# Messages of the tensor-product layer inside the first 100 turns of the ODE's loop

## The chip, the cores and the metric

The kernel runs on one core of a Trainium2 chip. A core has a matrix engine (TensorE, PE in the profile), VectorE (DVE), ScalarE (ACT), GpSimd (POOL) and SyncE (SP, which here only issues DMAs), each with its own queue of instructions, and semaphores between them. The metric is the device time of one execution in microseconds; of several runs the median counts.

## The reference

Eight layers follow each other, each with a layer norm ahead and a residual sum behind: graph convolution, experts, an equivariant tensor-product message layer, an ODE, a second graph layer, an LSTM, a third graph layer, and a product-key layer. `x` has 625 rows (nodes) of 512; there are 20000 edges, sorted by their receiver. The two layers that matter:

```python
# layer 3, for every edge: h is a small MLP of 8 edge features, y of 4 edge attributes
tpw = h @ W_mlp4 / sqrt(64)                     # 64 -> 512, split in w1..w4 of 128
s0, s1 = x0[sender], x1[sender]                 # 128, 128 x 3
p1 = w1 * s0 * y0
p2 = (w2 * s0)[:, :, None] * y1[:, None, :]
p3 = w3[:, :, None] * s1 * y0[:, None, :]
p4 = w4 * einsum('eum,em->eu', s1, y1) / sqrt(3)
msg = segment_sum([p1, p4, p2, p3], receiver)   # 1024 a node
x = x + lin(msg) / 10
# layer 4: y0 is row 0 of the normed x; 624 steps of Runge-Kutta 4, one row of output each
f = lambda z: tanh(tanh(z @ W1.T + b1) @ W2.T + b2) @ W3.T + b3
k1 = f(y); k2 = f(y + dt/2*k1); k3 = f(y + dt/2*k2); k4 = f(y + dt*k3)
y = y + dt * (k1 + 2*k2 + 2*k3 + k4) / 6
```

The ODE is one chain on a single row. It reads of layer 3's result only row 0; its own output is added to all rows.

## The kernel before

**Messages.** Nodes lie in NT = 5 groups of TN = 125, edges in 160 tiles of TE = 125, four to a unit of 500. `stage_graph` finds for each group the first unit and the number of units that hold its receivers (`bounds`); a unit on a border is worked through for both groups. With these inputs the five groups take 19, 8, 7, 5 and 5 units, 44 units of 4 = 176 tiles. `stage_messages` (L664) runs once per group, one after the other. SyncE loads the MLP's output for two tiles (L700), GpSimd copies the sender numbers (L710) and gathers the senders' 512 values by an indirect DMA (L713), TensorE makes `tpw` (L734: 64 rows contracted, 125 x 512 out, f32), VectorE forms the products and the one-hot matrix of receivers (L773 to L792), ScalarE p2 (L754), and TensorE adds up: one-hot times products, two times 512 columns into two banks that keep the sum over the whole group (L725). TensorE alternates, product of this tile, sum of the tile before. Behind the five stages `stage_message_out` (L799) transposes the sums and multiplies them by the output weights.

**ODE.** `layer_ode` (L877) first loads and multiplies weights, so that a step is done on the hidden side: `ps_z`, `ps_u` and `ps_a` are columns of 128 values, and `tanh` of one gives the input of the next product. A sub-step s = 0..3 has two halves, A (ScalarE: `a = tanh(ps_z or ps_u)`, L1034 or L1037; TensorE: `W2 a`, L1003) and B (ScalarE: `b = tanh(ps_a)`, L1039; TensorE: `M b`). Each product is split in four matmuls of 32 output rows (`quarters`, L980), since TensorE can take a column in four 32-wide tiles. Between the halves, where TensorE would wait for ScalarE, `busy` (L985) runs zero matmuls of 384 (A) or 320 (B) columns, two rounds of four quarters; nobody reads their result. VectorE adds `zh`, `zf` (L1049, L1050) from `ps_z`, which TensorE needs in the B half of s = 0, 1 and 2, and forms `part`, `p` and `sums` (L1052 to L1058); `p` is needed by TensorE in the B half of s = 3. A turn of the loop has UN = 4 steps (16 sub-steps), there are 156 turns. All is in the order in which it is written: every engine has one queue, nothing reorders. In the same block SyncE and GpSimd split the LSTM's weights into f16 parts in pieces of 1024 columns (`split_weights`, L1089), with nothing but their own waits between pieces.

## Time and profile before

| | us |
|---|---|
| median of 3 runs (8022.19 to 8033.26) | 8031.54 |
| the profiled execution, its span | 8021.68, 8020.0 |
| five message stages | 453 to 1047.9 |
| output product of the messages | 1047.9 to 1072.8 |
| the ODE's loop | 1105.0 to 3868.9 |
| TensorE busy, VectorE, ScalarE, GpSimd | 7173.6 (89%), 2471.2 (31%), 1713.7 (21%), 697.0 (9%) |

A line of a group names source line, engine, operation, output<-inputs, the tile of the matrix engine (rows*columns), the shape, the count, then busy time and the mean of one in ns, then the idle time ahead and what ended it. A matmul in f32 leaves two records. `PEclk` or the granted clock is given as a share of full speed, 1.00 being 2.4 GHz and 0.50 1.2 GHz. "Busy" of TensorE counts the zero matmuls too. PEld is the loading of weights, which runs ahead of the matmuls.

### The profile page before, as it was taken

Reading aid. Unit: us, or ns where it says so; the run is one execution under the profiler, and the core shown is the slowest. Engines: PE = TensorE matmul, PEld = TensorE weight load, DVE = VectorE, ACT = ScalarE, POOL = GpSimd, SP = SyncE. Lnnn points to the kernel's source line nnn. Section 1 sums busy time; section 2 is a strip of 40 time slices with the busy share of each in tenths; the row PEclk is TensorE's granted clock in tenths of the full one; section 3 lists DMA queues with packets and bytes.
Section 4 is the critical chain, followed back from the end, with each engine's and each line's share of the span. In section 5 each row is a group of like instructions: output and inputs, shape, how many; then the busy total and the mean of one; then the engine's idle time right before and its main releaser. Section 6 shows DMA issues by size and latency. Waiting matters only on the chain. (4 is left out here: it accounts for less than half of the span.)

```text
span 8020.0 us, 483127 instructions
## 1 busy us (share of the span) xinstructions
PE 7173.6 (89%) x209931; PEld 3982.8 (50%) x209931; DVE 2471.2 (31%) x12097; ACT 1713.7 (21%) x7668; POOL 697.0 (9%) x1191
## 2 busy tenths in 40 slices
PE   7889989999999999999798999999999999999851
PEld 5423244444444444444396555555555555555520
DVE  5267643211111111111243222222222222222247
ACT  0222222333333333333100111111111111111111
POOL 0134359100000000000000000000000000000000
PEclk9889999999999999999899999999999999999975
DMA  1133211000000000000031111111111111111100
GB/s 42 24 85 85 81 53 50 5 0 0 0 0 0 0 0 0 0 0 0 13 142 48 6 6 6 6 6 6 6 6 6 6 6 6 6 6 6 20 12 7
DMA packets 739824, 152.53 MB, mean 19 GB/s; under 512 B 694067, under 2 KB 708981, under 8 KB 739756
## 3 DMA queue, kind: packets, MB, share of 16 engines
q1 hardware_dynamic: 695596, 85.27, 7.2%
q0 software_dynamic: 40704, 45.90, 2.1%
q10 hardware_dynamic: 3456, 20.48, 0.6%
q8 instruction: 39, 0.64, 0.0%
q14 instruction: 29, 0.24, 0.0%
HBM read 123.19 MB, written 28.16 MB: 19 GB/s over the span
## 5 line engine op out<-in xcount | busy, mean ns | idle before, releaser
L988 PE MATMUL ode_busy<-ode_busy_x,ode_busy_w 128*32 128x320 f16 (+2 forms) x40000 | 2340.4, 311 | 44.7 <-issue 37.9
L1457 PE MATMUL ps_rows<-whh,h_pair 128*4 128x384 f16 x34944 | 1623.2, 326 | 18.6 <-issue 4.3
L1457 PEld LDWEIGHTS ps_rows<-whh,h_pair 128*4 128x4 f16 x34944 | 730.7, 84 | 698.4 <-issue 251.8
L982 PEld LDWEIGHTS ode_psa<-ode_a,ode_w2t 128*32 128x32 f32 x19968 | 410.4, 108 | 734.9 <-ACT ode_a L1037 578.9
L988 PEld LDWEIGHTS ode_busy<-ode_busy_x,ode_busy_w 128*32 128x32 f16 x40000 | 711.1, 95 | 57.1 <-issue 56.4
L1403 ACT COPY gate_rows<-ps_rows 128x384 f32<-128x384 f32 x624 | 298.3, 478 | 2057.6 <-PE ps_rows L1457 2057.6
L1378 DVE COPY gate_rows<-ps_rows_last 128x128 f32<-128x128 f32 x624 | 182.1, 292 | 1625.8 <-PE ps_rows_last L1457 1625.8
L1039 ACT ACTIVATE ode_b<-ode_psa 128x1 f32<-128x1 f32 x2496 | 427.2, 171 | 950.9 <-PE ode_psa L982 950.9
L982 PE MATMUL ode_psa<-ode_a,ode_w2t 128*32 128x1 f32 x19968 | 602.1, 180 | 0.0
L1037 ACT ACTIVATE ode_a<-ode_psu 128x1 f32<-128x1 f32 x1872 | 320.2, 171 | 726.4 <-PE ode_psu L982 726.4
L982 PE MATMUL ode_psa<-ode_ones,ode_b_parts 128*32 128x1 bf16 x9988 | 457.4, 163 | 0.0
L1052 DVE SCALAR_TENSOR_TENSOR ode_part<-ode_b 128x1 f32<-128x1 f32 x624 | 117.1, 188 | 932.0 <-ACT ode_b L1039 932.0
L1425 POOL COPY l_hist<-h_now 128x4 f32 x624 | 116.2, 186 | 3142.9 <-DVE h_now L1362 3142.9
L1457 PE MATMUL ps_rows_last<-whh,h_pair 128*4 128x128 f16 x19968 | 388.6, 219 | 0.0
L725 PE MATMUL msg_acc<-msg_m,msg_hot 125*125 125x512 f32 x724 | 372.1, 638 | 18.1 <-DVE msg_m L792 18.1
L1434 PE MATMUL lstm_busy<-lstm_busy_x,lstm_busy_w 128*128 128x512 f16 x1248 | 378.5, 385 | 0.0
L1457 PEld LDWEIGHTS ps_rows_last<-whh,h_pair 128*4 128x4 f16 x19968 | 330.7, 85 | 81.9 <-issue 0.5
L1504 PE MATMUL ps_gates<-l_gsel,gate_rows 128*32 128x4 f32 x19968 | 316.9, 178 | 54.1
L982 PEld LDWEIGHTS ode_psu<-ode_b,ode_mt_half 128*32 128x32 f32 x9984 | 223.2, 107 | 244.6 <-ACT ode_b L1039 210.6
L1504 PEld LDWEIGHTS ps_gates<-l_gsel,gate_rows 128*32 128x32 f32 x19968 | 262.0, 110 | 115.1 <-ACT gate_rows L1403 114.8
L982 PE MATMUL ode_psu<-ode_zh,ident 128*32 128x1 f32 x9984 | 287.3, 174 | 25.9 <-DVE ode_zf L1050 17.9
L1058 DVE TENSOR_TENSOR ode_sums<-ode_p,ode_b 128x1 f32 x624 | 137.3, 220 | 557.1 <-ACT ode_b L1039 554.5
(433 smaller groups left out, 8696.9 us busy)
## 6 DMA issues: line engine op xcount, KB each, us to landing
xg_buf<-xg_scratch SPq DMA_DIRECT2D x1248, 16.0 KB, 1.9
split_raw<-in_whh_t SPq DMA_DIRECT2D x32, 512.0 KB, 3.5
ig_w<-in_wih_t SPq DMA_DIRECT2D x8, 2048.0 KB, 10.6
xg_scratch<-ig_out ACTq DMA_DIRECT2D x16, 832.0 KB, 4.0
xg_scratch<-ig_out ACTq DMA_DIRECT2D x8, 836.0 KB, 3.6
msg_h<-h_scratch SPq DMA_DIRECT2D x88, 62.5 KB, 2.7
h_scratch<-mlp_h SPq DMA_DIRECT2D x40, 125.0 KB, 2.3
msg_snd<-up_scratch,msg_idx POOLq DMA_INDIRECT x176, 5.5
```

The lines of the kernel that those rows point to most:

```text
L725: mm = nc.tensor.matmul(acc[b][0:TN, :], hot[a % 2][:], m[a % 2][:, b * BANK:(b + 1) * BANK], start=False, stop=True, skip_group_check=True)
L982: m = nc.tensor.matmul(ps[32 * j:32 * j + 32, 0:1], w[:, 32 * j:32 * j + 32], col, start=start, stop=stop, skip_group_check=True)
L988: nc.tensor.matmul(ps_busy[32 * j:32 * j + 32, 0:cols], busy_w[:, 32 * j:32 * j + 32], busy_x[:, 0:cols], start=True, stop=True, skip_grou ...
L1037: nc.scalar.activation(a_col[:], ps_u[:, 0:1], ACT.Tanh).then_inc(S["a"], 1)
L1039: nc.scalar.activation(b_col[q][:, s:s + 1], ps_a[:, 0:1], ACT.Tanh).then_inc(S["b"], 1)
L1052: nc.vector.scalar_tensor_tensor(part[:], b_col[q][:, 1:2], 2.0, b_col[q][:, 0:1], ALU.mult, ALU.add).then_inc(S["s"], 1)
L1058: nc.vector.tensor_tensor(sums[:, ds(i * UN + (r + 1), 1)], psum_b[:], b_col[q][:, 3:4], ALU.add).then_inc(S["out"], 1)
L1378: nc.vector.tensor_copy(gsb[:, FIRST:D], psb[:, 0:D - FIRST]).then_inc(S["evac_v"], 1)
L1403: nc.scalar.copy(gsb[:, 0:FIRST], psg[:, e * BANK:e * BANK + FIRST]).then_inc(S["evac_a"], 1)
L1434: nc.tensor.matmul(ps_busy[:, 0:BANK], busy_w[:], busy_x[:, 0:BANK], start=True, stop=True)
L1457: m = nc.tensor.matmul(out[32 * j:32 * j + 4, :], hpair[:, c, 2 - 2 * part:6 - 2 * part], whh[:, at + lo:at + hi], start=(part == 0 and c ...
L1504: m = nc.tensor.matmul(psc[32 * j:32 * j + 32, c:16:4], gsb[:, c * 128 + 32 * j:c * 128 + 32 * j + 32], gsel[:], start=False, stop=(c == K ...
```

## The change

Units have two tiles instead of four (UNIT = 2*TE): 84 pairs of unit and group ("jobs") with these inputs, 168 tiles. A sixth group, ROW0, is voted for in `stage_graph`: the units that hold receivers of row 0 (4 with these inputs). `stage_jobs` computes two tables on VectorE, in some 70 short instructions: job -> tile, one-hot column, offset in `msg`. The first table holds the ROW0 jobs and whatever goes beyond 99 jobs; `stage_first_messages` runs these ahead of the ODE (which needs row 0), and `stage_message_out` is called for them alone ("fout"). The second table has SHADOW = 100 entries, one for each of the first 100 turns of the ODE's loop, its unused ones filled up with a job on unit 0 whose one-hot matrix is empty. In such a turn TensorE does one job, cut in 24 pieces of four f32 matmuls of 32 output rows (the last 29) by 128 columns. 16 pieces are sums (`sum_piece`), 8 are weights (`weight_piece`, 64 rows contracted, all others 125 or 128), in the order sums of tile 0 (pieces 0 to 7), weights of tile 1 (8 to 11), sums of tile 1 (12 to 19), weights of the next job's tile 0 (20 to 23). A piece stands at the head of the A half of every sub-step and of the B half of s = 0 and s = 3, in front of one round of zero matmuls of 256 (A) or 192 (B) columns; the B halves of s = 1 and s = 2 have no fill, in all 156 turns. The full "mout" output stage is called behind the ODE.

Further: `zh` and `zf` are made by ScalarE, behind `a` and `b` of s = 0. `ps_z` gets the b of each sub-step by a product of its own (a third matrix, `mt_third`), so TensorE no longer needs `p`. VectorE's sums (`step_sum`) may lag by four steps (`out`, waited for by ScalarE). In the first 100 turns VectorE makes the edge products between them (p2 too), and adds each job's sums to `msg`. The scratch of the messages lies in the buffer of the LSTM's weights, so the split, now in pieces of 512, stands in a second block with turns 100 to 155, whose fills are plain zero matmuls.

```diff
-UNIT = 4 * TE
+UNIT = 2 * TE
 UNITS = E // UNIT
+UT = UNIT // TE
+GROUPS = NT + 1
+SHADOW = 100
+JOBS = NT * UNITS
+FIRST_JOBS = UNITS + JOBS - (SHADOW - 1)
...
+def edge_products(nc, v, S, snd_in, B, ps_w, i, a, tile, column):
...
+    v.wait_ge(S["tpw"], i * UT + (UT + a + 1))
+    nc.vector.tensor_scalar(B["hot"][a], B["iota"][0:TE, ds(column, TN)], B["dst_f"][:, ds(tile + a, 1)], None, ALU.is_equal).then_inc(S["hot"], 1)
+    v.wait_ge(snd_in[a], i * 16 + 16)
+    nc.vector.tensor_scalar(dot, s1(0), y3_at(1), None, ALU.mult).then_inc(S["dot"], 1)
+    nc.vector.tensor_tensor(ws0, w(1), s0, ALU.mult).then_inc(S["ws0"], 1)
...
+    pairs = m[:, 2 * MUL:8 * MUL].rearrange("p (c k f) -> p c k f", c=3, k=2)
+    v.wait_ge(S["ws0"], i * UT + (a + 1))
+    for q in range(3):
+        nc.vector.tensor_scalar(pairs[:, q, 0, :], ws0, y_at(q + 1), None, ALU.mult).then_inc(S["out"], 1)
...
+def add_messages(nc, v, S, msg, acc, i, offset):
+    v.wait_ge(S["acc"], i + 1)
+    for b in range(2):
+        part = msg[:, ds(offset + b * BANK, BANK)]
+        last = nc.vector.tensor_tensor(part, acc[b][0:TN, :], part, ALU.add)
+    last.then_inc(S["added"], 1)
...
+        EDGE_QUARTERS = ((0, 32), (32, 64), (64, 96), (96, TE))
+        NODE_QUARTERS = ((0, 32), (32, 64), (64, 96), (96, TN))
+        def sum_piece(pe, i, a, c):
+            bank, at = acc[c // 4], (c % 4) * 128
+            if (a, c) == (0, 0):
+                pe.wait_ge(M["added"], i + 1)
+                pe.wait_ge(M["vec"], i * UT + 1)
+            for lo, hi in NODE_QUARTERS:
+                m = nc.tensor.matmul(bank[lo:hi, at:at + 128], B["hot"][a][:, lo:hi], B["m"][a][:, c * 128:(c + 1) * 128],
+                                     start=(a == 0 and c % 4 == 0), stop=(a == UT - 1), skip_group_check=True)
+            if c == 7:
+                m.then_inc(M["acc" if a else "summed"], 1)
+        def weight_piece(a, c):
+            for lo, hi in EDGE_QUARTERS:
+                m = nc.tensor.matmul(ps_w[a][lo:hi, c * 128:(c + 1) * 128], B["h3"][:, a * TE + lo:a * TE + hi], B["w4"][:, c * 128:(c + 1) * 128],
+                                     start=True, stop=True, skip_group_check=True)
+            if c == 3:
+                m.then_inc(M["tpw"], 1)
+        def job_piece(pe, i, n):
+            if n < 8:
+                sum_piece(pe, i, 0, n)
+            elif n < 12:
+                if n == 8:
+                    pe.wait_ge(M["vec"], i * UT + 2)
+                    pe.sem_inc(M["ready"], 1)
+                weight_piece(1, n - 8)
+            elif n < 20:
+                sum_piece(pe, i, 1, n - 12)
+            else:
+                if n == 20:
+                    pe.wait_ge(M["vec"], i * UT + (UT + 1))
+                    pe.sem_inc(M["ready"], 1)
+                    pe.wait_ge(M["h3_in"], i * 16 + 32)
+                    pe.sem_inc(M["ready"], 1)
+                weight_piece(0, n - 20)
+        def steps_tensor(pe, i, fill):
+            for r in range(UN):
+                k = i * (4 * UN) + 4 * r
+                b = b_col[r]
+                for s in range(4):
+                    fill(6 * r + (0, 2, 3, 4)[s], BUSY_A)
+                    pe.wait_ge(S["a"], k + (s + 1))
+                    quarters(ps_a, w2t, a_col[:], False, True).then_inc(S["wa"], 1)
+                    if s == 0:
+                        pe.wait_ge(S["zb"], i * (2 * UN) + (2 * r + 1))
+                        quarters(ps_u, ident, zh[:], True, False)
+                        fill(6 * r + 1, BUSY_B)
+                    elif s == 1:
+                        quarters(ps_u, ident, zh[:], True, False)
+                        pe.wait_ge(S["zb"], i * (2 * UN) + (2 * r + 2))
+                        quarters(ps_z, m0_parts, ones16[:], False, False)
+                        quarters(ps_z, mt_sixth, b[:, 0:1], False, False)
+                    elif s == 2:
+                        quarters(ps_u, ident, zf[:], True, False)
+                        quarters(ps_z, mt_third, b[:, 1:2], False, False)
+                    else:
+                        quarters(ps_z, mt_third, b[:, 2:3], False, False)
+                        fill(6 * r + 5, BUSY_B)
+                    pe.wait_ge(S["b"], k + (s + 1))
+                    if s < 3:
+                        quarters(ps_u, mt_full if s == 2 else mt_half, b[:, s:s + 1], False, True).then_inc(S["wu"], 1)
+                    else:
+                        quarters(ps_z, mt_sixth, b[:, 3:4], False, True).then_inc(S["wz"], 1)
+                    quarters(ps_a, b2_parts, ones16[:], True, False)
+        def steps_scalar(a, i):
+            for r in range(UN):
+                for s in range(4):
+                    if s == 0:
+                        a.wait_ge(S["wz"], i * UN + (r + 1))
+                        nc.scalar.activation(a_col[:], ps_z[:, 0:1], ACT.Tanh).then_inc(S["a"], 1)
+                        nc.scalar.activation(zh[:], ps_z[:, 0:1], ACT.Identity, bias=m0h[:]).then_inc(S["zb"], 1)
+                        a.wait_ge(S["out"], i * UN + (r + 1))
+                    else:
+                        a.wait_ge(S["wu"], i * (3 * UN) + (3 * r + s))
+                        nc.scalar.activation(a_col[:], ps_u[:, 0:1], ACT.Tanh).then_inc(S["a"], 1)
+                    a.wait_ge(S["wa"], i * (4 * UN) + (4 * r + s + 1))
+                    nc.scalar.activation(b_col[r][:, s:s + 1], ps_a[:, 0:1], ACT.Tanh).then_inc(S["b"], 1)
+                    if s == 0:
+                        nc.scalar.activation(zf[:], ps_z[:, 0:1], ACT.Identity, bias=m0f[:]).then_inc(S["zb"], 1)
...
+                with sp.Fori(0, SHADOW + 1) as i:
+                    tile = table_load(sp, table, 0, i, ET - UT)
+                    sp.wait_ge(M["tpw"], i * UT + UT)
+                    sp.dma_start(B["h3"], h3_dram[:, ds(tile * TE, UNIT)]).then_inc(M["h3_in"], 16)
+            @block.gpsimd
+            def _(g):
+                with g.Fori(0, SHADOW) as i:
+                    load_edges(nc, g, M, snd_in, B, up_dram, i, table_load(g, table, 0, i, ET - UT))
...
+                pe.sem_inc(M["tpw"], UT)
                 quarters(ps_z, ident, z0[:], True, True).then_inc(S["wz"], 1)
                 quarters(ps_a, b2_parts, ones16[:], True, False)
...
+                pe.wait_ge(M["h3_in"], 16)
+                for c in range(4):
+                    weight_piece(0, c)
+                with pe.Fori(0, SHADOW) as i:
+                    def fill(n, cols):
+                        job_piece(pe, i, n)
+                        busy(cols - 128, 1)
...
+                with v.Fori(0, SHADOW) as i:
+                    tile, column = table_load(v, table, 0, i, ET - UT), table_load(v, table, 1, i, NT * TN)
+                    offset = table_load(v, table, 2, i, (NT - 1) * 1024)
+                    step_sum(v, i, 0)
+                    v.wait_ge(M["summed"], i + 1)
+                    edge_products(nc, v, M, snd_in, B, ps_w, i, 0, tile, column)
+                    step_sum(v, i, 1)
+                    step_sum(v, i, 2)
+                    add_messages(nc, v, M, msg, acc, i, offset)
+                    edge_products(nc, v, M, snd_in, B, ps_w, i, 1, tile, column)
+                    step_sum(v, i, 3)
+        with nc.Block() as block:
+            @block.tensor
+            def _(pe):
+                with pe.Fori(SHADOW, STEPS // UN) as i:
...
+    stage_message_out(nc, "mout", msg, wo0_in, wo1_in, ident, x, x, range(NT))
```

On TensorE, a sub-step s = 1 of the ODE's loop, before (`ode_psa`, `ode_psu`, `ode_psz` are the columns, `ode_busy` the zero matmuls):

```order
L988 MATMUL ode_busy<-ode_busy_x,ode_busy_w 32x384 x8
L1002 REGISTER_ALU
L982 MATMUL ode_psa<-ode_a,ode_w2t 32x1 x4
L982 MATMUL ode_psu<-ode_zh,ident 32x1 x4
L988 MATMUL ode_busy<-ode_busy_x,ode_busy_w 32x320 x8
L982 MATMUL ode_psu<-ode_b,ode_mt_half 32x1 x4
L982 MATMUL ode_psa<-ode_ones,ode_b_parts 32x1 x4
```

and now, in the second step of a turn, where the piece is one of weights (`sm_psw<-whh`: the scratch is in the buffer `whh`):

```order
L1063 MATMUL ode_psu<-ode_b,ode_mt_half 32x1 x4
L1063 MATMUL ode_psa<-ode_ones,ode_b_parts 32x1 x4
L1100 REGISTER_ALU
L1089 MATMUL sm_psw<-whh 32x128 x3
L1089 MATMUL sm_psw<-whh 29x128
L1069 MATMUL ode_busy<-ode_busy_x,ode_busy_w 32x256 x4
L1121 REGISTER_ALU
L1063 MATMUL ode_psa<-ode_a,ode_w2t 32x1 x4
L1063 MATMUL ode_psu<-ode_zh,ident 32x1 x4
L1129 REGISTER_ALU
L1063 MATMUL ode_psz<-ode_ones,ode_m_parts 32x1 x4
L1063 MATMUL ode_psz<-ode_b,ode_mt_sixth 32x1 x4
```

A piece and one round of 256 columns stand where two rounds of 384 stood; the B half's fill is gone and two products into `ode_psz` are there, with a wait for `zf`.

On ScalarE, the begin of a step before:

```order
L1034 ACTIVATE ode_a<-ode_psz 128x1
L1038 ISA
L1039 ACTIVATE ode_b<-ode_psa 128x1
L1036 ISA
L1037 ACTIVATE ode_a<-ode_psu 128x1
```

and now:

```order
L1153 ACTIVATE ode_a<-ode_psz 128x1
L1155 ACTIVATE ode_zh<-ode_psz,ode_m0h 128x1
L1160 ISA
L1161 ACTIVATE ode_b<-ode_psa 128x1
L1163 ACTIVATE ode_zf<-ode_psz,ode_m0f 128x1
L1158 ISA
L1159 ACTIVATE ode_a<-ode_psu 128x1
```

The two additions, VectorE's before (L1049, L1050), stand behind the first two tanh.

## Rows read from the trace of the kernel before

**Rows 1.** Stretches: us, busy (instructions) by engine, TensorE's granted clock, DMA share, GB/s.
```profile
30.00:122.00 92.00, 84.60 (x887) 67.09 (x888) 81.90 (x355) 4.25 (x9) 0.00 (x0) 0.98 0.13 40
458.00:1046.00 588.00, 558.49 (x1091) 179.84 (x1090) 416.77 (x1423) 173.74 (x528) 244.49 (x349) 0.96 0.32 86
1105.00:1445.00 340.00, 311.29 (x12828) 160.37 (x12824) 112.82 (x357) 97.54 (x570) 309.93 (x160) 0.98 0.16 47
2500.00:3200.00 700.00, 688.33 (x28740) 342.70 (x28736) 112.13 (x799) 218.49 (x1277) 0.00 (x0) 1.00 0.00 0
```

**Rows 2.** Timeline in the ODE: start, us, engine, instruction [idle before <- releaser].
```profile
1600.18 0.45 PE L988 MATMUL ode_busy<-ode_busy_x,ode_busy_w 128*32 128x320 f16 x8
1600.35 0.17 ACT L1039 ACTIVATE ode_b<-ode_psa 128x1 f32<-128x1 f32 x1 [0.36 <-PE ode_psa L982]
...
1600.68 0.50 PE L988 MATMUL ode_busy<-ode_busy_x,ode_busy_w 128*32 128x384 f16 x8
1600.88 0.17 ACT L1037 ACTIVATE ode_a<-ode_psu 128x1 f32<-128x1 f32 x1 [0.36 <-PE ode_psu L982]
...
1602.15 0.16 DVE L1049 TENSOR_TENSOR ode_zh<-ode_psz,ode_m0h 128x1 f32<-128x1 f32 x1 [0.28 <-ACT ode_a L1034]
...
1603.08 0.17 ACT L1037 ACTIVATE ode_a<-ode_psu 128x1 f32<-128x1 f32 x1 [0.42 <-PE ode_psu L982]
...
1607.10 0.17 ACT L1039 ACTIVATE ode_b<-ode_psa 128x1 f32<-128x1 f32 x1 [0.65 <-PE ode_psa L982]
```

**Rows 3.** Groups by line, 458 to 1046 us: busy us, mean ns | idle before.
```profile
L725 PE MATMUL msg_acc<-msg_m,msg_hot 125*125 125x512 f32 x724 | 372.1, 638 | 18.1 <-DVE msg_m L792 18.1
...
L725 PEld LDWEIGHTS msg_acc<-msg_m,msg_hot 125*125 125x125 f32 x724 | 124.7, 192 | 251.0 <-issue 224.7 <-DVE msg_m L792 26.3
L788 DVE SCALAR_TENSOR_TENSOR msg_m<-msg_psw,tp_y,msg_snd 125x384 f32<-125x384 f32 x176 | 107.5, 611 | 0.0
...
L792 DVE TENSOR_TENSOR msg_m<-msg_psw,msg_dot 125x128 f32<-125x128 f32 x176 | 49.2, 279 | 0.0
...
L760 DVE MEMSET msg_m<- 125x1024 f32 x4 | 3.6, 912 | 7.6 <-issue 7.6
```

**Rows 4.** Timeline at both ends of the message stages and of the output stage.
```profile
453.05 3.77 PE L720 MATMUL msg_acc<-tp_zeros 128*125 128x512 f32 x4 [16.28 <-PEq L863]
...
462.18 0.29 DVE L778 TENSOR_SCALAR msg_dot<-msg_snd,tp_y 125x128 f32<-125x128 f32 x1 [6.45 <-DMA msg_snd<-up_scratch,msg_idx]
...
1047.89 0.91 SPq L85 DMA_DIRECT2D out_w<-in_L_gnn_W_out  x2
...
1072.14 0.65 DVE L847 SCALAR_TENSOR_TENSOR x_rows<-out_pso,x_rows 125x384 f32<-125x384 f32 x1
```

**Rows 5.** Timeline in the ODE while GpSimd splits the LSTM's weights.
```profile
1299.12 2.07 DVE L1052 SCALAR_TENSOR_TENSOR ode_part<-ode_b 128x1 f32<-128x1 f32 x1 [1.67 <-ACT ode_b L1039]
...
1301.44 0.24 PE L982 MATMUL ode_psz<-ode_p,ode_mt_sixth 128*32 128x1 f32 x8 [0.43 <-DVE ode_p L1055]
```

**Rows 6.** Page: a weight load of the ODE, and the gathers' issue and landing.
```profile
L982 PEld LDWEIGHTS ode_psa<-ode_a,ode_w2t 128*32 128x32 f32 x19968 | 410.4, 108 | 734.9 <-ACT ode_a L1037 578.9
...
msg_snd<-up_scratch,msg_idx POOLq DMA_INDIRECT x176, 5.5
```

**Rows 7.** Timeline of TensorE in the message stages.
```profile
639.64 1.12 PE L734 MATMUL msg_psw<-tp_w,msg_h 64*125 64x512 f32 x2
640.70 1.98 PE L725 MATMUL msg_acc<-msg_m,msg_hot 125*125 125x512 f32 x4
```

**Rows 8.** ScalarE's timeline, then the stretch 1134 to 1135 us, in the ODE.
```profile
1132.64 0.17 ACT L1037 ACTIVATE ode_a<-ode_psu 128x1 f32<-128x1 f32 x1 [1.74 <-PE ode_psu L982]
...
1134.45 0.17 ACT L1039 ACTIVATE ode_b<-ode_psa 128x1 f32<-128x1 f32 x1 [0.57 <-PE ode_psa L982]
...
1134.00:1135.00 1.00, 1.00 (x45) 0.76 (x44) 0.16 (x1) 0.17 (x1) 0.75 (x1) 0.50 0.00 0
```

**Rows 9.** Timeline of TensorE in the LSTM.
```profile
5001.14 0.22 PE L1487 MATMUL ps_gates<-xg_buf,ident 128*32 128x16 f32 x8
```

More of the change, by code:

```diff
@@ new lines, in message_semaphores, with stage_first_messages, bound @@
+def message_semaphores(nc, tag):
+    S = {k: new_semaphore(nc, f"{tag}_{k}") for k in ("tpw", "hot", "dot", "ws0", "out", "vec", "acc", "added", "idx", "seen", "cleared", "h3_in", "ready", "summed")}
+    return S, [new_semaphore(nc, f"{tag}_snd_in{a}") for a in range(UT)]
+def stage_first_messages(nc, up_dram, h3_dram, B, first_table, first_count, msg):
+    S, snd_in = message_semaphores(nc, "fm")
+    with ExitStack() as ctx:
+        ps_w = [ctx.enter_context(nc.psum_tensor(f"fm_psw{a}", [128, BANK], F32)) for a in range(UT)]
+        acc = [ctx.enter_context(nc.psum_tensor(f"fm_acc{a}", [128, BANK], F32)) for a in range(2)]
+        def bound(eng):
+            return eng.snap(eng.value_load(first_count[0:1, 0:1], min_val=1, max_val=FIRST_JOBS), min_val=1, max_val=FIRST_JOBS)
@@ L693, in _ @@
             def _(sp):
-                first, count = bound(sp, j, 0, first_max), bound(sp, NT + j, 1, count_max)
-                with sp.Fori(0, count) as i:
-                    unit = nc.s_assert_within(first + i, 0, first_max, skip_runtime_bounds_check_because="first + count is at most the number of units")
-                    for b in range(T // 2):
-                        sp.wait_ge(S["tpw"], i * T + (2 * b + 2))
-                        sp.dma_start(h3[b][:], h3_dram[:, ds(unit * UNIT + b * (2 * TE), 2 * TE)]).then_inc(h3_in[b], 16)
+                with sp.Fori(0, bound(sp)) as i:
+                    tile = table_load(sp, first_table, 0, i, ET - UT)
+                    sp.wait_ge(S["tpw"], i * UT + UT)
+                    sp.dma_start(B["h3"], h3_dram[:, ds(tile * TE, UNIT)]).then_inc(S["h3_in"], 16)
@@ L739, in _ @@
[L739 to L755 removed]
+                pe.sem_inc(S["tpw"], UT)
@@ new lines, in _ @@
+                pe.sem_inc(S["acc"], 1)
+                with pe.Fori(0, bound(pe)) as i:
+                    pe.wait_ge(S["h3_in"], i * 16 + 16)
+                    for a in range(UT):
+                        pe.wait_ge(S["vec"], i * UT + (a + 1))
+                        nc.tensor.matmul(ps_w[a][0:TE, :], B["h3"][:, a * TE:(a + 1) * TE], B["w4"], start=True, stop=True).then_inc(S["tpw"], 1)
+                    pe.wait_ge(S["added"], i + 1)
+                    for a in range(UT):
+                        pe.wait_ge(S["vec"], i * UT + (UT + a + 1))
+                        for b in range(2):
+                            m = nc.tensor.matmul(acc[b][0:TN, :], B["hot"][a], B["m"][a][:, b * BANK:(b + 1) * BANK], start=(a == 0), stop=(a == UT - 1))
+                    m.then_inc(S["acc"], 1)
@@ L794, in _ @@
[L794 to L808 removed]
+                nc.vector.memset(msg[:], 0.0).then_inc(S["cleared"], 1)
@@ new lines, in _ @@
+                v.wait_ge(S["cleared"], 1)
+                v.sem_inc(S["vec"], UT)
+                v.sem_inc(S["added"], 1)
+                with v.Fori(0, bound(v)) as i:
+                    tile, column = table_load(v, first_table, 0, i, ET - UT), table_load(v, first_table, 1, i, NT * TN)
+                    offset = table_load(v, first_table, 2, i, NT * 1024)
+                    for a in range(UT):
+                        edge_products(nc, v, S, snd_in, B, ps_w, i, a, tile, column)
+                    add_messages(nc, v, S, msg, acc, i + 1, offset)
@@ L812, in _ @@
             def _(pe):
-                for i in range(NT):
+                for i, t in enumerate(tiles):
                     for b in range(2):
@@ L831, in _ @@
             def _(a):
-                for i in range(NT):
+                for i, t in enumerate(tiles):
                     if i >= 2:
@@ new lines, in build @@
+        end_of_layer(nc)
+        layer_ode(nc, x, x_first, ident, ones, B, (up_dram, h3_dram, table, msg, a["L1_gnn_W_out0"], a["L1_gnn_W_out1"]),
+                  a["L1_ffn_W1T"], a["L1_ffn_b1"], a["L1_ffn_W2T"], a["L1_ffn_b2"], a["L1_ffn_b2_row"], a["L1_ffn_W3"], a["L1_ffn_W3T"],
+                  a["L1_ffn_b3T"], a["L1_ffn_b3"], a["whh_t"], whh)
+        end_of_layer(nc)
+        messages.close()
+        if "sage" in stages:
+            layer_mean(nc, x, ident, adj, rcount, a["L2_gnn_WT"], a["L2_gnn_b"])
+            end_of_layer(nc)
```

463 lines of the change are left out of this document (227 added, 236 removed).

## The prediction

> **What bounds the kernel now.** I went from the coarse view to the fine one. The table of stretches [rows 1] comes first: in 458 to 1046 us, the message stages, TensorE is busy 558.5 of 588 us, and in the ODE (1105 to 3869) it is busy 98 % of the time at a granted clock of 1.00. The two are busy in different ways, and the change rests on that. In the ODE, most of the work is filler: zero matmuls at L988 whose result nobody reads. What sets the pace there is a chain between ScalarE and TensorE [rows 2]: one tanh of 0.17 us, 0.36 us until TensorE's product releases the next one, so 0.533 us for a half of a sub-step (1600.35 to 1600.88). In the messages the matmuls are real work; the groups by line [rows 3] show 724 records of L725 alone for 176 tiles. So 595 us of real work (453 to 1047.9, where the next stage loads, [rows 4]), 3.4 us a tile, stand in front of 2764 us in which TensorE mostly turns over zeros, and the change puts the one inside the other. What has to be priced is whether the chain of 0.533 us notices.
>
> **How a turn of before is made.** A turn of the loop has four steps of eight halves, 32 x 0.533 = 17.06 us. The B half of s=0 waits 0.06 us more in three of the four steps (0.42 instead of 0.36 at 1603.08, [rows 2]), because TensorE waits there for zh and zf from VectorE, and the turn's end costs 0.65 - 0.36 = 0.29 us once (1607.10). Together 17.53 us. The table of stretches gives the same: 1277 ScalarE instructions in 700 us, 8 to a step, is 4.385 us a step, 17.54 a turn [rows 1].
>
> **What goes.**
> 1. The five message stages: -595 us. Of the 176 tiles [rows 3], 44 units of four, units of two leave 84 jobs (168 tiles) by the inputs' edges; 84 is under the 99 that the schedule holds, so only the jobs with row 0 (4 of them, by the inputs) run ahead of the ODE.
> 2. Two waits of the ODE on VectorE. zh and zf come from ScalarE, in the 0.36 us in which it waits anyway: 3 x 0.06 = 0.18 us a turn, 156 turns, -28 us.
> 3. The delay by the split of the weights. In 1105 to 1445, with GpSimd busy 309.9 of 340 us, a step takes 340 / (570/8) = 4.77 us, 0.387 more than later, times 71 steps: 27.5 us. The cause is at 1299.12 [rows 5]: a VectorE instruction of 0.16 us takes 2.07 us beside GpSimd's, and TensorE then waits 0.43 us for ode_p, with ScalarE's next tanh behind it. Afterwards TensorE needs nothing from VectorE but a sum four steps old (ScalarE's wait on "out"), and the split runs in the last 56 turns, 982 us for some 340 of work. -27 us.
>
> **What is added ahead of the ODE.** Four first jobs: a memset of 6144 columns at 0.91 per 1024 (L760, [rows 3]) is 5.5 us; 7 us until the first gather has landed (VectorE waits 6.45 us at 462.18, [rows 4]); then 10 us a job, since with one buffer a tile the next gather starts when the tile's products are done (5.5 us of landing [rows 6], and about two for the copy of the index and the issue), and a tile's own products take about 3. With an overlap at the first one: +52. Job tables: about 71 short instructions in a row on VectorE, each waiting for the one before; no such chain is in the trace. At 0.16 us (VectorE's L1049 on one column, 1602.15 [rows 2]) they are 11 us, at 0.28 to 0.3 (128 columns, L792 [rows 3]) plus as much as 0.15 for the wait 31; they work on 5 to 100 columns, so I take +24, nearer the upper end. The row-0 tile through the output product: the stage's 25 us (1047.89 to 1072.8, [rows 4]) hold a load and five tiles; one tile with the load is between 5 and 25, and I take 11. The full output stage itself is moved behind the ODE, +-0. Graph stage with two tiles a turn instead of four: 92 us now [rows 1], VectorE 82 of them, so it is VectorE's rate and not the ring that counts; +3. Extra load, votes, one more program block between turns 100 and 101: +6. Together +96 us, between 70 and 130.
>
> **What is added in the first 100 turns.** This is the term that decides. 24 halves of the 32 in a turn get a piece: four f32 matmuls of 32 output columns and 128 streamed ones, beside fewer zeros. A further f32 record of 512 columns takes 0.43 us (a group of two is 1.12 us long, of four 1.98, [rows 7]), two records to a matmul, so 128 columns take 0.21; if the four quarters stream side by side, a piece is 0.21 us. The A fill was 768 columns; its group of eight is 0.05 longer than the B fill's for 128 columns more [rows 2], 0.42 ns a column, so 0.32 us; it is now 0.21 + 256 columns (0.11) = 0.32: nothing. The B fill was 640, 0.27 us, and becomes 0.21 + 192 (0.08) = 0.29, but only in two of four halves, and the other two have none. TensorE's slack: the A fill starts at 1600.68, has streamed by 1601.00 and the next tanh releases at 1601.05 plus the 0.05 of a start, so 0.10 us; for the B fill 0.12. So the sum pieces (16 a turn) are hidden. TensorE's queue in the front part's excerpt shows it: a sum piece, its 192 columns, and then the quarters that wait for ScalarE.
>
> The 8 weight pieces a turn are another matter. They contract over 64 rows (64*125 in L734's tile), everything around them over 125 or 128. In [rows 7] the two forms alternate: from the start of the one at 639.64 to the start of the other at 640.70 it is 1.06 us, where two records of one form need 0.86. So a change of rows costs 0.20 us there. Part of it may be the weight load, which is 0.19 us for 125 columns (L725 PEld, [rows 3]) and 0.108 for 32 (L982, [rows 6]), and which may hide wholly beside a neighbour of the same form. A weight piece is followed by zeros of 128 rows, so each such fill holds two changes: up to 2 x 0.20 - 0.10 of slack = 0.30 us late, at the least nothing. I take the middle, 0.15, as the load is about half as long: 8 x 0.15 = 1.2 us a turn, +120 us, bounds 0 and +240.
>
> [...]
>
> VectorE has to do a job in a turn: two tiles at 3.1 us (hot, and eleven products of 0.28 to 0.61 each that overlap in part [rows 3], three of them ScalarE's before), two additions of 512 columns (1.4), twelve instructions for the sums (2.4) and some loads (1.5): 11.7 of 17.5 us. The gathers have 5.5 + 2 us and a turn's better half to land in. Cover is there, but the waits of pieces 0, 8, 12 and 20 on VectorE are now on TensorE's queue, with the chain's quarters behind them; where I put the times of a turn side by side, the nearest has some 1.6 us to spare. +10 us for what of it is late and for the loads of job numbers in the queues, between 0 and 60.
>
> **Sum**, against the profiled execution's 8021.7 us: -595 - 28 - 27 + 96 + 120 + 10 = 7597.7. The profiled execution is 10 us under the median of the runs shown (8031.5), so 7600 to 7608; I say 7600.
>
> **The rivals.**
> *A. The change of rows costs nothing in 32-column tiles.* For it: the weight load of 125 columns is half of the 0.20. Against: a load of 32 columns is still 0.108, and the neighbour's price need not be one of loading. Then 7600 - 120 = 7480.
> *B. The clock falls besides.* The trace has such places in the ODE: at 1134 to 1135 the granted clock is 0.50, that is 1.2 GHz, after ScalarE, and with it the chain, had stood 1.74 us behind VectorE at 1132.64; the halves take 0.57 + 0.17 = 0.74 us instead of 0.533 [rows 8], and it comes back within four or five halves, a loss of about 0.9 us. Two B halves of four have no zeros now, and a late weight piece leaves a gap; once a turn would be +90: 7690.
> *C. Slower: the quarters of a piece run one after another.* The trace has no f32 matmuls of 32x128 tiles with different weights and data. If TensorE gives them no common time, a piece takes 4 x 0.21 = 0.86 instead of 0.21, the half is 0.65 - 0.10 = 0.54 us late, 2400 times: +1300 us, near 8800. It decides from 0.2 us a fill on (some 430 us of gain without the fills, over 2400, plus the slack's part). Against it: eight records of f32 in 32-column tiles take 0.22 us together in the LSTM [rows 9], and the zeros' quarters run side by side.
> *D. Slower: the clock stays at 1.2 GHz in the 100 turns.* 3200 halves x 0.2 = +640: 8240. Against: the busy share hardly falls, and where it dropped before it came back by itself. [...]
> That the messages don't run in the ODE at all (everything left in the first stage) is excluded by 84 under 99.
>
> **Chances.** The sum above 0.45 (7540 to 7660 by its own terms), A 0.25, B 0.17, C 0.04, D 0.03, and 0.06 for a wait in the schedule that I have not seen and that eats some hundreds of us of the gain: 0.04 of it still faster, 0.01 even, 0.01 slower. 8 in 10 need the first three: 7450 (A with cheap tables) to 7730 (B, or the upper bound of the changes of rows). What can be told from no change is 0.2 %, 16 us; faster 0.91, within 0.01, slower 0.08.
>
> **What would show it.** The half with a weight piece (A of s=1, 2, 3 and B of s=3 in steps 2 and 4) takes 0.68 us, those with a sum piece 0.533. A turn takes about 18.7 us in the first 100 and 17.36 after them, also beside the split. The ODE's first step begins near 606 us. I am wrong if the time is gained back in waits of TensorE for VectorE (msg_m) in front of a piece, if all halves with pieces are longer (C), or if the clock column of the first 100 turns is under 0.95 (B, D).

## The result, and the profile after

The changed kernel takes 9093.25 us (median), 1.133 times before (95% interval 1.1307 to 1.1357); 7600 was forecast. The profiled execution has a span of 9089.7 us.

| us | before | forecast | after |
|---|---|---|---|
| graph stage | 121.2 | +3 | 171.4 |
| job tables; first messages | | 24; 52 | 24.0; 60.0 |
| first step of the ODE begins | 1105.0 | 606 (581 by the terms of the sum) | 630.1 |
| a turn, mean of the first 100 | 17.82 | 18.7 | 32.93 |
| a turn, mean of the last 56 | 17.54 | 17.36 | 17.60 |

(The 606 forgot that the output stage's 25 us move behind the ODE. In before, the first 18 turns run beside the split of the weights; the others take 17.54.) The miss of 1493 us is in the first 100 turns: 100 x (32.93 - 18.7) = 1423. Of the rest, 49 us lie ahead of the ODE. Stretches of after, columns as in [rows 1]:

```profile
1000.00:2000.00 1000.00, 751.90 (x24936) 565.47 (x24928) 268.41 (x1098) 204.45 (x1223) 85.61 (x122) 0.56 0.09 22
...
4000.00:5000.00 1000.00, 894.00 (x37585) 489.65 (x37572) 156.07 (x681) 356.88 (x2093) 278.04 (x262) 0.95 0.05 16
```

The last row of [rows 1] had TensorE 98% busy at 1.00; with the messages beside the chain it is 75% busy at 0.56, near the lower level, 0.50 in [rows 8]. The profile gives the clock only as a share of full speed. What stands for the GHz of the recorded texts is this: in before the A fill of 768 columns takes 0.50 us at 1.00 (1600.68, [rows 2]) and 0.82 us at 0.50 (1134.97), 0.32 us more (the B fill of 640 takes 0.45 and, at 1134.33, 0.71). With twice the time a column at half the clock that is 0.42 and 0.83 ns a column, 2.4 and 1.2 columns a ns; at one column a cycle it would be 2.4 and 1.2 GHz, an estimate from these times. 1223 ScalarE instructions at 40 a turn are 30.6 turns. TensorE waits, but for what? Groups on the page, and the waits of 1000 to 2000 us (in total, times, longest):

```profile
L1081 PE MATMUL ode_pso<-whh 125*32 125x128 f32 (+1 forms) x12800 | 1089.8, 397 | 613.1 <-issue 612.8
```
```profile
PE ode_pso L1081 <- issue: 183.5, 68, 4.8
PE sm_psw L1089 <- issue: 20.3, 19, 1.7
```

"issue" means that nothing was being waited for: no semaphore of VectorE, which was the forecast's fear. The stands come twice a turn:

```profile
2009.97 0.65 PE L1081 MATMUL ode_pso<-whh 125*32 125x128 f32 x8 [4.43 <-issue]
...
2010.95 0.17 ACT L1161 ACTIVATE ode_b<-ode_psa 128x1 f32<-128x1 f32 x1 [4.18 <-PE ode_psa L1063]
...
2012.90 0.42 PE L1081 MATMUL ode_pso<-whh 125*29 125x128 f32 x1 [1.43 <-issue]
```

The first one stands at the head of a turn, before piece 0, which does wait for VectorE. But VectorE's last product for it had ended 6 us earlier:

```profile
2003.57 0.28 DVE L770 TENSOR_TENSOR whh<-sm_psw,whh 125x128 f32<-125x128 f32 x1
```

The second stand is in the middle of a piece, where no semaphore is waited for. The DMA queues of 2000 to 3000 us name what moves meanwhile (packets, MB, share):

```profile
q0 software_dynamic: 13664, 15.69, 5.9%
q8 instruction: 276, 4.52, 2.1%
```

276 packets of 16 KB are 9.0 a turn. In all, the page has

```profile
q8 instruction: 935, 15.32, 0.8%
```

where before had 39 packets, and none in that stretch. So the reading is that TensorE fetches the code of the loop again in every turn; the packets don't name an engine, and e9 below tests it. The rest of a turn is at the low clock (granted 0.50 in 2001 to 2004 and in 2014 to 2020), seen on ScalarE: the tanh of a half with a weight piece waits 0.83 us, where [rows 2] has 0.36.

```profile
2002.98 0.17 ACT L1161 ACTIVATE ode_b<-ode_psa 128x1 f32<-128x1 f32 x1 [0.83 <-PE ode_psa L1063]
```

### The profile page after: what moved, and what is told of

The parts are those of the page before. It is cut to its first block and busy times, and to the rows that moved or that the text cites. A ratio compares the mean times of both kernels' runs of the same rounds, so it can differ in the third digit from the quotient of the medians.

```text
span 9089.7 us, 502643 instructions
## 1 busy us (share of the span) xinstructions
PE 7367.4 (81%) x218499; PEld 4865.8 (54%) x218499; DVE 2642.5 (29%) x11980; ACT 1730.8 (19%) x8390; POOL 774.1 (9%) x1417
## 5 line engine op out<-in xcount | busy, mean ns | idle before, releaser
L1069 PE MATMUL ode_busy<-ode_busy_x,ode_busy_w 128*32 128x384 f16 (+2 forms) x20416 | 1713.1, 346 | 21.4 <-issue 13.7
L1081 PE MATMUL ode_pso<-whh 125*32 125x128 f32 (+1 forms) x12800 | 1089.8, 397 | 613.1 <-issue 612.8
L1063 PEld LDWEIGHTS ode_psa<-ode_a,ode_w2t 128*32 128x32 f32 x19968 | 683.7, 136 | 357.3 <-ACT ode_a L1159 216.9
L1069 PEld LDWEIGHTS ode_busy<-ode_busy_x,ode_busy_w 128*32 128x32 f16 x20416 | 590.3, 109 | 341.9 <-issue 319.1
L1081 PEld LDWEIGHTS ode_pso<-whh 125*32 125x32 f32 (+1 forms) x12800 | 397.4, 143 | 698.5 <-issue 698.1
L1063 PE MATMUL ode_psa<-ode_a,ode_w2t 128*32 128x1 f32 x19968 | 697.8, 191 | 0.9 <-ACT ode_a L1153 0.4
L1570 DVE COPY gate_rows<-ps_rows_last 128x128 f32<-128x128 f32 x624 | 182.0, 292 | 1625.9 <-PE ps_rows_last L1649 1625.9
L1089 PE MATMUL sm_psw<-whh 64*32 64x128 f32 (+1 forms) x6432 | 466.6, 377 | 62.1 <-issue 60.7
L1063 PE MATMUL ode_psu<-ode_b,ode_mt_half 128*32 128x1 f32 x9984 | 360.8, 192 | 44.7 <-ACT ode_b L1161 5.6
L1063 PEld LDWEIGHTS ode_psu<-ode_b,ode_mt_half 128*32 128x32 f32 x9984 | 306.7, 134 | 152.3 <-ACT ode_b L1161 103.0
L1063 PEld LDWEIGHTS ode_psa<-ode_ones,ode_b_parts 128*32 128x32 bf16 x9988 | 365.5, 117 | 0.0
```

The source lines that it names most:

```text
L1063: m = nc.tensor.matmul(ps[32 * j:32 * j + 32, 0:1], w[:, 32 * j:32 * j + 32], col, start=start, stop=stop, skip_group_check=True)
L1069: nc.tensor.matmul(ps_busy[32 * j:32 * j + 32, 0:cols], busy_w[:, 32 * j:32 * j + 32], busy_x[:, 0:cols], start=True, stop=True, skip_grou ...
L1081: m = nc.tensor.matmul(bank[lo:hi, at:at + 128], B["hot"][a][:, lo:hi], B["m"][a][:, c * 128:(c + 1) * 128], start=(a == 0 and c % 4 == 0) ...
L1089: m = nc.tensor.matmul(ps_w[a][lo:hi, c * 128:(c + 1) * 128], B["h3"][:, a * TE + lo:a * TE + hi], B["w4"][:, c * 128:(c + 1) * 128], star ...
L1570: nc.vector.tensor_copy(gsb[:, FIRST:D], psb[:, 0:D - FIRST]).then_inc(S["evac_v"], 1)
```

## The experiments

All were compared with before on the same chip (8027 to 8032 us); runs without an interval are one execution each. "Turn" is the mean of the first 100, from ScalarE's first tanh of turn 0 to that of turn 100; the length of a "half" is a median over these turns. The edits are against after unless said otherwise.

**First round: where is it lost?**

e1 (against before): three rounds of zeros instead of two.
```diff
-busy(BUSY_A)
-busy(BUSY_B)
+busy(256, 3)
+busy(213, 3)
```


> The kernel before, its zero matmuls cut finer: A fill 3 rounds of 256 columns instead of 2 of 384, B fill 3 of 213 instead of 2 of 320. Same columns, same chain, no messages in the ODE, but 128 more matmuls in a turn: TensorE's loop body grows from about 1460 to about 1720 instructions (two for each f16 matmul, four for each f32 one); the changed kernel's has about 1660. Theory 1 (the loop's code no longer stays loaded: each turn is fetched anew, TensorE stands at the start of the turn): some 9 instruction packets of 16 KB a turn and 6 us of TensorE's standing a turn, so 156 x 6 = 940 us or more slower, near 8970, with the clock falling to 0.5 to 0.6 in the ODE. Theory 2 (the f32 pieces or their different rows cause the loss, code has no part): within 30 us of 8020.


8034.2: no loss, and 40 instruction packets in all. By the trace, TensorE's queue holds 1719 instructions a turn here (848 matmuls, as many weight loads, 23 others) and 1666 in after (816, 816, 34). The longer body fetches nothing, so the number of instructions alone doesn't decide.

e3: no zeros beside a piece.
```diff
-                        busy(cols - 128, 1)
```


> The changed kernel without the zero matmuls beside the pieces; all messages stay. TensorE's body in the first 100 turns is about 1470 instructions, what the last 56 turns have (about 1470, and those ran without fetching). Theory 1 (code): no instruction packets in the first 100 turns, the two stands of 4.4 and 1.9 us a turn are gone, at least 630 us faster than the changed kernel, 8460 or less; if the clock stays at 1.2 GHz for want of zeros, near 8400, if it rises to 2.4 GHz, near 7550. Theory 2 (the f32 pieces keep TensorE slow): a few us a turn at most from the missing zeros, near 9000.


7951.0, faster than both kernels; turn 21.52. Clock 0.50 in all of the 100 turns at 97% busy, no fetching:
```profile
1000.00:1500.00 500.00, 485.53 (x16796) 314.60 (x16788) 202.41 (x837) 155.95 (x933) 64.96 (x93) 0.50 0.10 27
```
At a granted clock of 0.50 a half with a sum piece takes 0.58 us without zeros; in after it takes 0.77 to 0.80. So zeros, meant to keep the clock up, cost 0.2 us a half once it is down.

e4: each piece one 125x125 matmul.
```diff
-            for lo, hi in NODE_QUARTERS:
-                m = nc.tensor.matmul(bank[lo:hi, at:at + 128], B["hot"][a][:, lo:hi], ...
+            m = nc.tensor.matmul(bank[0:TN, at:at + 128], B["hot"][a], ...
```


> The changed kernel with each piece as one matmul of 125 output rows instead of four of 32, so the same 128 columns stream, the zero matmuls stay, and the body has about 1375 instructions. Theory 1 (code): no fetching, the clock at 1.00, and a turn of 17.4 us plus what 24 changes to whole tiles and back cost: at most 24 x (2 x 0.2 - 0.1) = 7 us, so between 7480 and 8200; I say 7700. Theory 2 (f32 pieces): as slow as the changed kernel or slower, 9000 or more.


9050.0, turn 32.45, at a clock of 0.50 and without fetching, where 7700 was expected. The piece and the zeros behind it run one after the other, and the load of the next form waits 0.22 us; every half with a piece takes 1.15 us.
```profile
1201.32 0.79 PE L1080 MATMUL ode_pso<-whh 125*125 125x128 f32 x2
...
1202.03 0.11 PEld L1069 LDWEIGHTS ode_busy<-ode_busy_x,ode_busy_w 128*32 128x32 f16 x4 [0.23 <-issue]
```

e5: no messages in the 100 turns, plain fills (the work of these jobs is left out).
```diff
-                    steps_tensor(pe, i, fill)
+                    steps_tensor(pe, i, lambda n, cols: busy(cols))
```


> The changed kernel with all message work of the 84 jobs left out of the first 100 turns (no pieces, no gathers, no products on VectorE); these turns have zero matmuls like the last 56. It leaves that part of the messages uncomputed. It shows what all the rest of the change costs: by my sum 8022 - 595 + 96 - 28 - 27 = 7470 with a turn of 17.36 us throughout, also beside the split. If it is over 7550, the order of the ODE's own products or the stages ahead of it cost more than I said.


7584.1, turn 17.56. What isn't the pieces cost 114 us more than the sum without its two piece terms had it: the graph stage +47, first messages +8, the turns +33 (item 6 below), and the LSTM stage, 3296.0 instead of 3264.8 with the same code.

**Second round: what of the pieces does it?** e6, e7, e10, e11, e13 and e16 have no message work in the 100 turns; in e6 each piece is four zero matmuls, f32, 128 rows x 32 x 128 columns, in e7 four f16 ones of 512 columns.
```diff
-                        job_piece(pe, i, n)
+                        for j in range(4):
+                            nc.tensor.matmul(ps_busy[32 * j:32 * j + 32, 0:128], zero_w[:, 0:32], zero_x[:, 0:128], ...)
```


> The changed kernel without message work in the ODE (it leaves that part uncomputed), but with each piece replaced by one of the same shape over zeros, f32, four quarters of 32 x 128, beside the same zeros in f16: TensorE's loop has the same 320 f32 and 176 f16 matmuls, no waits on VectorE, no gathers. Theory 1 (f32 pieces count for less than the f16 zeros they replace, so the clock falls to 1.2 GHz): clock 0.50 to 0.6 in the first 100 turns, as in the changed kernel, 8350 to 9000. If the instruction packets come too (9 a turn), code size is their cause and not the waits. Theory 2 (the clock falls because TensorE waits for VectorE's products and the gathers): clock near 0.98, 7600 or less.

> As the run before, but the piece is f16 over 512 columns, which streams as long as 128 columns of f32 (0.21 us); again without message work in the ODE. Theory 1: clock 0.96 or more, a turn of 17.4 to 17.6, so 7560 to 7600. Theory 2b (any change of what is streamed, or the shorter fill, lowers the clock): as slow as the f32 one.


7570.8 and 7583.4; turn of e6 17.49, no fetching, a granted clock of 1.00:
```profile
1000.00:1500.00 500.00, 461.66 (x23440) 330.72 (x23436) 55.11 (x345) 192.06 (x1149) 0.00 (x0) 1.00 0.00 0
```
The same number and type of matmuls as after, in tiles of the same width, cost nothing; TensorE has 1659 instructions a turn, 7 fewer than after. Rival C is out, and so is that f32 pieces pull the clock down.

e8 (against e3): 512 columns of zeros in the B halves of s = 1 and 2.


> The changed kernel with all its messages, no zeros beside the pieces, but one round of 512 f16 columns in each of the 8 B halves of a turn that had no fill. TensorE's loop is still shorter than the changed kernel's (320 f32 and 112 f16 matmuls), so I expect no fetching. The run without any zeros gave 21.46 us a turn at 0.50. Theory 1: 4096 columns a turn are not enough to bring the clock back, so 0.50 again and 21.5 to 22 us a turn (at 1.2 GHz a round takes 0.43 us and the gap is about that): 7950 to 8000. If the clock does come back, a turn of 18 to 19 us and 7650.


8143.3, more than either theory had: each such half 0.72 to 0.75 instead of 0.58, and the clock stays down (0.54).

e9: zeros beside the sum pieces only.
```diff
-                        busy(cols - 128, 1)
+                        if n < 8 or 12 <= n < 20:
+                            busy(cols - 128, 1)
```


> The changed kernel, zeros beside the 16 sum pieces only, none beside the 8 weight pieces: 320 f32 and 144 f16 matmuls in a turn instead of 320 and 176, all messages stay. Theory 1 (code that just doesn't fit): no instruction packets in the loop, the stands of 4.4 and 1.9 us a turn are gone, and 8 halves are shorter by one round at 1.2 GHz (0.21 us) as well, with the clock still at 0.50: 9093 - 630 - 100 or so, 8300 to 8450. Rival (the fetching is not a matter of size): still 9 packets a turn and near 9000.


8264.0, turn 24.65, 44 instruction packets in all, and the stands are gone, though pieces and waits are the same. Taking 32 of 176 f16 matmuls out of the turn (1602 instructions are left) took 829 us away; by the lengths of the halves no more than 8 x 0.2 = 1.6 of the 8.3 us a turn are the zeros themselves. The rest goes with the fetching. What starts it is not shown: after has 1666 instructions a turn, e6 1659 and e1 1719, and after alone fetches. Where the loop's code begins was not varied.

**Third round: who takes the clock?** e10 is e6 with the eight weight pieces over 64 rows, e11 with real weights, e13 with 125 rows and 29 columns, e12 is e9 with `w4` and `h3` padded to 128 rows.
```diff
+rows = 64 if 8 <= n < 12 or n >= 20 else 128
-..., zero_w[:, 0:32], zero_x[:, 0:128], ...
+..., zero_w[0:rows, 0:32], zero_x[0:rows, 0:128], ...
```


> The run with zero f32 pieces (7570.8, clock 0.956), but the 8 pieces that stand where the weight pieces were contract over 64 rows instead of 128; still zeros, still no message work in the ODE (that part is left uncomputed). It tells whether the change of rows is what holds the clock down and what it costs. Theory R (rows): the clock falls to 0.50 to 0.6 and the time goes to 8100 or more. Theory D (the values that are streamed, not the shape): clock 0.95 or more, and a fill with 64 rows is late by 0.1 to 0.3 us, so 7650 to 7800, or 7571 if the change of rows costs nothing here.

> The run with zero f32 pieces (7570.8), but the pieces multiply the ODE's own matrices (128 x 128, f32, not zero) instead of zeros; same shapes of 32 x 128 over 128 rows, result unread. It leaves the message work in the ODE uncomputed. Theory D (values): clock 0.50 to 0.6 and 8100 or more, though nothing else differs. Theory R (rows): as with zeros, 7560 to 7600.

> The run with zero f32 pieces (7570.8), with all pieces over 125 rows and the last quarter of 29 columns, as the sum pieces of the changed kernel are; zeros, no message work in the ODE (left uncomputed). If the odd shapes of the pieces hold the clock down: 0.50 to 0.6 and over 8100. Otherwise 7560 to 7600; that is what I expect.

> The changed kernel with zeros beside the 16 sum pieces only (8264.0 us, clock 0.5 in the first 100 turns), but its weight pieces contract over 128 rows, 64 of them zeros, so that no piece has other rows than its neighbours. All messages stay. Theory R: the clock comes up to 1.00 and a turn takes 17.5 us, near 7600. Theory D: the clock stays at 0.50 and only the 0.23 us go by which a weight half is longer than a sum half at 1.2 GHz: 8 x 0.23 x 100 = 180 us less, near 8080.


8103.4, 7575.2, 7568.7 and 8136.7. Among the zero kernels only the 64 rows count: +533 us. At a granted clock of 1.00 (1199 to 1201) such a half takes 0.65 instead of 0.53 us, as the wait ahead of the zeros' weights shows,
```profile
1200.60 0.42 PE L1189 MATMUL ode_busy<-ode_busy_x,ode_busy_w 64*32 64x128 f32 x8
...
1200.95 0.10 PEld L1069 LDWEIGHTS ode_busy<-ode_busy_x,ode_busy_w 128*32 128x32 f16 x4 [0.20 <-issue]
```
which is 8 x 0.12 = 1 us a turn. But the turn is 5.3 us longer: behind these halves the clock goes down (0.76 in 1201 to 1202, 0.50 in 1202 to 1203), and then halves with a piece take 0.77 to 0.80, those with 64 rows 1.01. In some turns it comes back before the next weight pieces, in others not at all; the mean is 0.64:
```profile
1000.00:1500.00 500.00, 479.37 (x17856) 381.70 (x17847) 41.62 (x262) 146.33 (x875) 0.00 (x0) 0.64 0.00 0
```
In the real kernel the rows are not enough: e12 is 127 us under e9, and its clock is 0.59 (theory R had 1.00 and 7600).

**Fourth round: e12's rest.** e14 (against e12) puts the zeros beside other pieces (`if n % 12 >= 4: busy(cols, 1)`); e15 (against e12) has no gathers, VectorE works on constants; e16 is e6 with the two gathers a turn and nothing else.


> The changed kernel with weight pieces over 128 rows (as the run of 8136.7), and with its 16 rounds of zeros placed otherwise: none beside the first four sum pieces of a tile, which is where GpSimd's gathers are issued, a round of 384 or 320 columns beside each other piece. All messages stay. In the run of 8136.7 TensorE's product stood about 1 us where a gather's issue (1.22 us on GpSimd) met a product behind zeros, while in the kernel without zeros no such stand was seen. Theory G (a gather's issue holds up the zero matmuls, the late product leaves TensorE with too little to do, and the clock falls): no stands over 1.2 us, clock over 0.9 in the first 100 turns, a turn of 17.5 to 19 us, so 7570 to 7750. Rival (the clock falls because of something else in the real messages): the clock stays near 0.58 and the time over 8000.

> The run of 8136.7 without the gathers of the first 100 turns: the senders' rows are a constant, so the messages are not the reference's; all products, sums and waits stay. Theory G: the stands of 1 us at the turn's halves 2 and 18 are gone, the clock is over 0.9, and the time 7570 to 7700. Rival (VectorE's products or the pieces' waits hold the chain): 8000 or more, the clock near 0.58.

> The run with zero f32 pieces (7570.8, no message work in the ODE, which stays uncomputed) with the two gathers a turn added on GpSimd and nothing else: no products, no real pieces, nobody waits for the gathers. Theory G: 200 stands of the chain of 0.5 to 1.2 us at the gathers' issues, each followed by some low clock: 7700 to 8100. Rival: 7571 to 7590.


8190.3, 7871.5 and 7989.0. So moving the zeros doesn't help: in e14 the half at the second gather still takes 1.7 us. The gathers alone (with the copy of the sender numbers ahead of each) cost 418 us. One issue holds GpSimd for 1.22 us, and over it ScalarE stands, for a product that by the profile, where ends of matmuls are modelled, TensorE ran in 1877.68 to 1877.96. Its result is taken only when the issue is over (in e12):
```profile
1877.59 1.22 POOL L789 DMA_INDIRECT whh<-up_scratch,whh  x1 [0.91 <-POOL whh L786]
1877.68 0.28 PE L1065 MATMUL ode_psu<-ode_b,ode_mt_half 128*32 128x1 f32 x8
...
1878.88 0.17 ACT L1161 ACTIVATE ode_a<-ode_psu 128x1 f32<-128x1 f32 x1 [1.41 <-PE ode_psu L1065]
```
In e16 a half of 1.5 us at the second gather is followed, four halves later, by five of 0.77 to 0.80. In e15 the rest, 300 us over e6, begins where one turn of the loop follows another: that half takes 1.18 us, in e6 0.84; why is not shown. Why the gathers of e3 hold the chain less stays open too.

**Last round: the way out.** e17: e12 without any zeros beside the pieces. e18: besides, the graph stage's loops take pairs of units again, with bounds in pairs and four buffers. e19 (against before): two pairs of hot buffers.
```diff
-        hot_s = [sb(f"hot_s{r}", [TE, N], F16) for r in range(RING)]
+        hot_s = [sb(f"hot_s{r}", [TE, N], F16) for r in range(2)]
```


> The kernel after, with the weights and h3 of a message held as 128 rows (the 64 added ones are zero), and no zero matmul beside a piece. Nothing is left uncomputed. Theory (the clock stays at 1.2 GHz in the 100 turns without zeros, so a gather's stall costs no clock more; the change of rows is paid at each weight piece beside its half): with 64 rows this arrangement took 7951 us, with sum halves of 0.58 and weight halves of 0.82 us; at 128 rows the 16 weight halves fall by 0.1 to 0.2 us each, 1.6 to 3.2 us a turn, so a turn near 19.3 and 7630 to 7790 us, say 7740. Rival (the weight half is long through its 108 ns loads of f32 pieces, not through the rows): 7950 as before. Both theories see no code fetching.

> The kernel of the last run, with the graph's loops again over four tiles a turn and four pairs of hot buffers (bounds in pairs of units, made by eleven more small VectorE operations). Nothing is left uncomputed. Theory (the graph stage's 50 us more, 121.2 to 171.4, are the ring of two buffers and the doubled number of loop turns): the stage back near 123 us and the whole 46 to 50 us below the last run. Rival (the stage is longer by the added group's votes and other work of the change): less than 15 us.

> The kernel before, with two pairs of hot buffers in the graph stage's ring in place of four; the loop's four tiles a turn stay. Nothing is left uncomputed. Theory A (the ring of two alone makes the stage longer, since VectorE can't run ahead over TensorE's loop turn): graph stage 160 to 170 us, 8072 to 8080 in all. Theory B (the doubled number of loop turns does it, with their register loads and branches): 121 to 125 us, 8032.


- e17: 7846.1, ratio 0.977 (0.9757 to 0.9783), 105 under e3. The halves with weight pieces fell from 0.82 to 0.58 as expected, but three others rose, the most at the second gather, from 0.70 to 1.04; turn 20.43 where 19.3 was expected, and 7846 where 7740 was.
- e18: 7809.7, ratio 0.9725 (0.9712 to 0.9738), the best version. The graph stage is back at 123.1 us, 48 less; only 36 arrive, since the LSTM stage took 3299.5 us where e17 had 3271.4, with the same code in it. That is unexplained.
- e19: 8083.6, ratio 1.0062 (1.0047 to 1.0078), graph stage 182.0. The ring of two alone makes the stage longer, without one more turn of the loop, and by more than was expected (160 to 170). After's VectorE shows it, idle before the one-hot matrices for TensorE (L276):
```profile
L224 DVE TENSOR_SCALAR hot_s<-iota_h,src_f 125x625 f16<-125x625 f16 x168 | 65.4, 389 | 48.9 <-PE ps_adj L276 37.6 <-PE ps_adj L269 11.3
```

## Why the prediction was wrong

The sum gave the pieces 130 us (+120 for the change of rows, +10 for waits), 1.3 us a turn over 17.36. Measured are 32.93 - 17.36 = 15.6 us a turn. Items 2 to 4 are the steps that failed.

1. *The five message stages, -595, and the sum pieces "hidden": right by themselves.* e6 shows that 24 pieces of 128 rows in 32-column tiles fit beside the chain: 17.49 us a turn, 17.36 forecast.
2. *The step that failed* is the one on weight pieces, "I take the middle, 0.15 ... bounds 0 and +240", with the clock kept apart from it as rivals B and D. The 0.15 was good (0.12 measured in e10). What it sets off was not in the term: behind the late halves the granted clock goes to 0.50 (1202 to 1203 in e10), and there the fill of piece and zeros no longer fits into the half. e10: +533 us instead of +120. Rival B had the clock back "within four or five halves" [rows 8], as before's trace has it (0.50 in 1134 to 1136, 0.52 in the next us, 1.00 from 1137 on); but in e10 each following fill is late by itself, and the clock is down for about 70% of the 100 turns (0.65 granted). The argument against D, that the clock had come back by itself, failed with it: D, given 0.03, had the clock right (0.56 in after). Its price, 0.2 us a half or 6.4 us a turn, is near the 7.2 that e9 pays over e6; e3, without zeros, pays 4.0. The prediction's "98 % at a granted clock of 1.00" for the whole loop is the row of 2500 to 3200 us; that of 1105 to 1445 has 92% at 0.98 [rows 1].
3. *A rival that was missing:* nothing in the forecast counted the code of a turn. Fetching is worth about 670 to 830 us (e9 against after), about half of the miss. A count of instructions would have raised the question, but not settled it: after, with 1666 instructions a turn, takes 9.0 packets a turn (276 for 4.52 MB in 2000 to 3000 us), and e1, with 1719, has 40 in all. What size or place of the code starts the fetching no run shows.
4. *"+10 for waits"* took GpSimd's gathers as free, as their data lands in time. The data does land in time; it is the issue that isn't free (e16, +418). The waits on VectorE that the forecast feared are not seen.
5. *"VectorE's rate and not the ring ... +3":* +50. VectorE was busy 82 of 92 us, but it got there by running up to four tiles ahead while TensorE's loop turned (e19).
6. *Two waits gone, -28, and the split's delay, -27:* right for most turns, but only 22 of the 55 us came. In e5, without messages, the median turn is 17.35, and the whole loop takes 2741.6 us where before took 2763.4: every six to ten turns the half at the turn's head takes 1.0 to 1.2 us instead of 0.83, and the turn 18.3 or 19.0. The split itself no longer delays: 17.35 a turn beside it, where before had 4 x 4.77 = 19.1.

The parts don't add up: e10, e15 and e16 each bring 3.3 to 5.3 us a turn over e6, and together, in e9, 7.2; each of them pays in part through the same low clock (in 1000 to 1500 us granted 0.64, 0.70 and 0.78, and 0.54 in e9). So the shares of the four causes (fetching, rows, gathers, and what is left in e15) in the 1423 us are not separable beyond this: about half is fetching, and half is the low clock with what sets it off.

## What to carry to other kernels

Work put in the gaps of a latency-bound chain has to be counted three times: its columns at full clock, its columns at the low one, since a few late halves can bring the chain there (eight a turn of 0.65 instead of 0.53 us, granted clock 0.65 over the 100 turns of e10), and its instructions, since a loop can begin to fetch its code in every turn; the profile's instruction packets show it (935 in after, 39 in before). Zeros that are meant to keep the clock up are dead weight once it is down (0.2 us a half at 0.50, e3 against after): here the version without them, and with all matmuls over the same number of rows, won (e17). When a unit is halved, look at every ring whose depth was the unit.

## What the runs showed of the hardware that was not expected

- Removing 32 matmuls of a turn that has 496 turned 9 instruction packets a turn into none, and 32.9 us into 24.7 (e9); a body with 53 more instructions than after's had none (e1). The price came as a step, and where the step lies is not a matter of their number alone.
- By the profile TensorE was 97% busy in e3's 100 turns and was granted 0.50 throughout; e6, 92% busy, had 1.00.
- The issue of an indirect DMA of 125 rows holds GpSimd for 1.22 us, and the chain between ScalarE and TensorE, which needs nothing from it, can stand about 1 us over it.
- Between 64 and 128 rows, the next weight load waits 0.20 us at a granted clock of 1.00 in 32-column tiles too (e10); in [rows 7] the change of rows cost the same 0.20 us at 512 columns. Between 125 and 128 rows nothing was lost (e13).
